# Leaving out the unread TensorE products at the tile edges of an LSTM and mixture-of-experts kernel

## The reference, cut to what matters

```python
def step(carry, xw_t):                       # L0: 1024 steps, one after the other
    prev_h, prev_c = carry
    a = xw_t + prev_h @ Wh                   # [2, 256] @ [256, 1024]
    i, f, o = sigmoid(three quarters of a); g = tanh(the last quarter)
    next_c = f * prev_c + i * g
    next_h = o * tanh(next_c)
x = x + hs
# L1: 2 shared experts, 8 routed experts of which the router takes 2 per token
shared = mean_e((silu(x @ s_w1[e].T) * (x @ s_w3[e].T)) @ s_w2[e].T)
routed = sum_e(gelu(x @ r_w1[e].T) @ r_w2[e].T * gate[:, e])
x = x + (shared * 2 + routed) / 4            # in effect; all ten experts are computed
```

## Time and profile before

| | |
|---|---|
| timed runs, median (lowest to highest) | 1907.95 us (1906.42 to 1908.26), 3 runs |
| the profiled execution's own time | 1904.1 us |
| its span, first to last instruction | 1902.3 us |
| mean granted TensorE clock over the span | 0.997 |
| TensorE products | 1818.4 us busy (96%), 45672 records |
| TensorE weight loads | 1609.8 us busy (85%) |
| VectorE | 1540.1 us busy (81%) |
| ScalarE | 851.9 us busy (45%) |
| GpSimd | 123.4 us busy (6%) |

### The profile page before, as it was taken

The page is one execution under the profiler, slowest core; times in us unless marked ns, Lnnn a source line. Parts: engine busy times, 40 slices in busy tenths (PEclk is TensorE's granted clock), DMA queues, the critical chain, the costliest instruction groups (busy, mean ns, idle before and its releaser), DMA issues. The chain is left out here.

```text
span 1902.3 us, 111519 instructions
## 1 busy us (share of the span) xinstructions
PE 1818.4 (96%) x45672; PEld 1609.8 (85%) x45672; DVE 1540.1 (81%) x13274; ACT 851.9 (45%) x5545; POOL 123.4 (6%) x409
## 2 busy tenths in 40 slices
PE   8999999999999999999999999999999999999998
PEld 7888888888888888888888888888888888888887
DVE  7788888788888878888788888888888788887884
ACT  4564444444444444444444444444444444444442
POOL 0000000000000000000000000000000000000000
PEclk9999999999999999999999999999999999999999
DMA  6000000000000000000000000000000000000000
GB/s 247 4 3 4 4 6 4 7 4 4 6 4 7 4 4 7 4 7 4 7 4 4 7 4 7 4 4 7 4 7 4 7 4 4 7 4 6 4 4 7
DMA packets 7282, 20.86 MB, mean 11 GB/s; under 512 B 1136, under 2 KB 5616, under 8 KB 5872
## 3 DMA queue, kind: packets, MB, share of 16 engines
q1 hardware_dynamic: 6768, 13.73, 1.9%
HBM read 11.63 MB, written 2.10 MB: 7 GB/s over the span
## 5 line engine op out<-in xcount | busy, mean ns | idle before, releaser
L734 PE MATMUL gates<-hh,wh_hi 128*128 128x24 f16 x8192 | 784.9, 183 | 0.0
L734 PE MATMUL gates<-hh,wh_lo 128*128 128x24 f16 x8192 | 784.9, 183 | 0.0
L734 PEld LDWEIGHTS gates<-hh,wh_hi 128*128 128x128 f16 x8192 | 550.8, 96 | 0.0
L734 PEld LDWEIGHTS gates<-hh,wh_lo 128*128 128x128 f16 x8192 | 549.6, 95 | 0.0
L333 ACT ACTIVATE gates<-gates 128x4 f32<-128x4 f32 x1024 | 161.8, 158 | 839.3 <-DVE gates L597 822.4
L716 PEld LDWEIGHTS gates<-hh,wh_lo 128*128 128x128 f16 x8192 | 274.1, 96 | 276.1 <-DVE hh L623 270.2
L742 PE MATMUL gates<-hh,wh_small 128*128 128x2 f16 x8192 | 489.6, 164 | 0.0
L716 PE MATMUL gates<-hh,wh_lo 128*128 128x24 f16 x8192 | 381.3, 185 | 73.0 <-DVE hh L623 10.5
L597 DVE TENSOR_TENSOR_SCAN gates<-part_fac,gates 128x8 f32<-128x8 f32 x2048 | 294.4, 178 | 168.0 <-PE gates L723 141.1
L723 PE MATMUL gates<-hh,wh_hi 128*128 128x4 f16 (+1 forms) x8192 | 370.4, 171 | 0.0
L742 PEld LDWEIGHTS gates<-hh,wh_small 128*128 128x128 f16 x8192 | 350.0, 96 | 0.0
(11 more groups left out here) (144 smaller groups left out, 2575.5 us busy)
## 6 DMA issues: line engine op xcount, KB each, us to landing
rw_sb<-rw SPq DMA_DIRECT2D x2, 2048.0 KB, 22.3
sw_sb<-sw SPq DMA_DIRECT2D x3, 1024.0 KB, 12.8
outT<-osb SPq DMA_DIRECT2D x16, 128.0 KB, 2.2
x_sb<-xT SPq DMA_DIRECT2D x1, 1920.0 KB, 8.9
wh_sb<-wh SPq DMA_DIRECT2D x1, 1024.0 KB, 4.8
wx_sb<-wx SPq DMA_DIRECT2D x1, 1024.0 KB, 6.3
x_sb<-xT SPq DMA_DIRECT2D x1, 128.0 KB, 4.6
eye_sb<-eye SPq DMA_DIRECT2D x1, 64.0 KB, 5.1
```

The lines of the kernel that those rows point to most:

```text
L734: mm(copies(q, m, LOW_COPIES)[:, :, :, 1], part, hh[:, c, half:half + 1, :].broadcast_to([P, LOW_COPIES, B]), start=False, stop=False, ski ...
```

## The change

The table `EDGE`, the helper `beside_up` and its call are taken out. Nothing else is altered: the same waits, the same order, the same other products.

```diff
 BETWEEN = (5, 8, 11, 14)
-EDGE = {0: 2, 1: 3, TS - 1: 3}
...
-            def beside_up(n):
-
-                for j in range(n):
-                    mm(up_sh[:, TT:BANK], wh_hi[:, 0, j * P:(j + 1) * P], wh_hi[:, 1, 0:BANK - TT], start=True, stop=True)
-
...
                 for s in range(TS):
                     lstm(s, it)
                     mixture(s, True)
-                    if s in EDGE:
-                        beside_up(EDGE[s])
                 take_back(pe, s_hhi, TS)
```

## The result

The change makes the kernel slower: 1921.03 us median of 4 runs (1918.28 to 1922.62) against 1907.24 us of the kernel before beside them (4 runs, 1906.42 to 1908.26), ratio 1.007 with a 95% interval of 1.0057 to 1.0083. 1915.8 us were predicted, with a range of 1905.2 to 1928. The profiled execution took 1922.29 us, its span is 18.2 us longer than the one before, and its mean granted clock is 0.978 instead of 0.997.

The account below looks back on a forecast made before the run. The prediction took each step's round through the engines, not TensorE alone, as the bound. Removing the products gains 2.2 us and half clock costs 10.1 us: +7.9 us, 1915.8 us with the timed offset, range 1905.2 to 1928.

Parts of the forecast that it names:

- What bounds the kernel: Each of 1024 steps is one round through the engines, 1.79 us; TensorE work ending before the next `hh` costs nothing.
- The direct gain: At 15 tile edges, removing step 1's three unread products saves 0.15 us each, 2.2 us; steps 63 and 0 give nothing.
- The price of a piece: A piece is 3.41 us of TensorE at half clock; priced at 0.84 us from a stretch in tile 0.
- The number of pieces: Half-clock stretches of 3.41 us newly expected around the 15 edges: 12, within 0 to 30, costing 10.1 us.
- Both sentences among the rivals on a second piece: At an edge, thinner half-clock steps favour a second 3.41 us half-clock stretch; float32 groups from step 2 on oppose it.
- The likeliest case: 8 to 22 half-clock stretches of 3.41 us, net of the 2.2 us gain: 1911.7 to 1924 us.
- The rival without a fall: Gate products alone keep TensorE's clock up at the edges; only 2.2 us gained, 1905.7 us; chance 0.22.
- Few falls: Only some edges lose the clock, 1 to 7 half-clock stretches, net -1.4 to +3.7 us, 1906.6 to 1911.6 us; chance 0.08.
- long falls everywhere: Two 3.41 us half-clock stretches at every edge, 30 in all, 1930.9 us; chance 0.10 for nearly every edge.
- The faster rival: Step 63's unread products also delay step 0 at each edge; 0.32 us per edge, 4.8 us, 1903.1 us; chance 0.04.

Follow-up runs that it names:

- e6: Kernel before with six instead of three unread products in step 1 of each edge; 1912.97 us, ratio 1.0045.
- e1: Kernel before without the three unread products of step 1 at each edge; 1902.01 us, ratio 0.9986.
- e2: Kernel before without the three unread products of step 63 at each edge; 1905.46 us, ratio 1.0002.
- e3: Kernel before without the two unread products of step 0 at each edge; 1905.16 us, ratio 1.0001.
- e7: Kernel before without step 1's unread products, plus eight 384-column unread products behind step 34 of tile 0; 1903.24 us, ratio 0.9991.
- e4: Kernel before with all eight unread products per edge cut from 384 to 24 columns; 1915.86 us, ratio 1.0067.
- e8: Kernel before with all eight unread products per edge cut from 384 to 192 columns; 1904.11 us, ratio 0.9999.
- e11: Kernel before with only step 63's three unread products kept at each edge; 1910.40 us, ratio 1.0017.
- e9: Kernel before with only step 0's two unread products kept at each edge; 1903.69 us, ratio 0.9996.
- e10: Kernel before without step 1's unread products, with unread 384-column products added at three waits (tile 0 start, step 34, behind tile 15); 1899.83 us, ratio 0.9971.
- e12: Kernel before with only step 1's three unread products kept at each edge; 1918.21 us, ratio 1.0046.

## Why the prediction was right, point by point

**What bounds the kernel: right.** The round of a step sets the pace. Work on TensorE in the gap is free up to 0.34 us beyond the logits in step 1 and costs one to one after that (e6).

**The direct gain, 0.15 us per edge from step 1 alone: right.** -0.20 and -0.13 us at the two edges of the kernel after that kept the clock, and 1.78 or 1.79 us instead of 1.94 for the step at all 15 edges of e1. The groups of steps 63 and 0 cost nothing, by e2 and e3.

**The price of a piece, 0.84 us: right at the edges, wrong in the tail.** An edge with one piece is 0.68 us longer, that is 0.83 with the 0.15 gained; one with two 1.44 us, 1.59 with it, or 0.80 a piece. The two pieces behind tile 15 cost 2.7 us, 1.4 each. In all traces what follows the last L623 takes 36.7 us without a piece, 37.9 to 38.2 with one, 39.2 to 39.4 with two. There the mixture runs alone, and I read the higher price as that of TensorE setting the pace itself, which no run tries. I had priced all pieces by a stretch of the recurrence. Its fourth step takes 1.86 us even at full clock (e7), so the piece there was 0.80 us rather than 0.84.

**The number of pieces, 12: too small, and this is the term that was mis-sized.** The profiled execution has 21: 19 at the edges (7 x 0.83 + 6 x 1.59 = 15.3 us) and two in the tail. With them 15.3 + 2.7 - 2.2 = 15.8 us; 1.3 us of longer set-up and 0.4 in tile 0 are the rest but 0.7. Between the medians it is 13.8 us where 7.9 were forecast. The 12 weren't derived but chosen between 0 and 30; that the time fell inside the range is owed to the range's width as much as to the mechanism. Both sentences among the rivals on a second piece had a share in it: six of 13 edges had two, where the fall came early and half clock lay over steps 0 to 2, and seven had one, where it came late and step 2's float32 groups followed. Nearly every edge fell, too, though in the profiled execution the first two did not. The likeliest case was put at 1911.7 to 1924 us for 8 to 22 pieces; by its own prices 8 pieces are 1912.5.

**The rival without a fall: wrong.** It rested on busy time, 1.87 us or more against 1.81. The fall at 606 us came after 2.19 us of work in 3.40, more than the 2.10 us that were not followed by one in the earlier trace rows. The one at 493.40 us came after 2.88 us. Busy time doesn't tell; what the runs show is that eight products of 24 columns left falls at six edges where eight of 384 or 192 columns left none (e4, e8). The rule of the Trainium skill (TensorE: Matmul & The Clock Gate, "Why this matters for your kernels") that leads to this rival, that a long idle gap brings the clock down, doesn't account for these falls: the longest gap ahead of the one at 606 us was 0.79 us, ahead of the one at 489.85 us in e11 it was 0.43, and e2 had 0.79 without a fall.

**Few falls, long falls everywhere, faster: none came.** 1930.9 us would have needed two pieces at every edge. The faster rival needed the group of step 63 to delay the tile's end; e2 excludes it.

**Open.** Why edges 1 and 2 of the profiled execution kept their clock while the later ones lost it was not tried; the runs at clock 0.976 to 0.980 say that others have some more or fewer pieces. That e7, e8 and e9 gain less in time than their steps show is put down to the tail and the set-up of the profiled executions only. Which of its two effects kept the clock in e7, and so in tile 0 of e10, is open.

## What to carry to other kernels

An unread product can earn its place on an engine that isn't the bound, because that engine's products are in the round that is, and they take longer at half clock. Ask of such filler how wide it is and where it stands: two wide products in the middle of the light stretch did here what eight narrow ones didn't, and what three at either end of it didn't. Ask also what stands right behind it: the last group cost 0.16 us for each product that ended too late, and more when the clock was down. Before taking filler out, look for the pieces at half clock that the trace has already and read their price there, once where the engine is waited for and once where it sets the pace.

## What the runs showed of the hardware

- A loss that isn't additive. Any one of the three groups can go for nothing; two can go if step 0's stays (e1, e2, e3, e9: 0.9986 to 1.0002); with all gone it is 13.8 us.
- A pattern that feeds itself. From edge 4 on the falls of the kernel after alternate, one piece, two pieces, one piece, and the stretches with two begin at 601.89, 833.99, 1066.09, 1298.19 and 1530.29, each 232.10 us after the last. In before two tiles take 229.9 us. In e12 every second edge falls, from the third on. I read this so: a fall lengthens the tile and with it moves the next edge against the throttle. No run shifts an edge by itself to show it. Either way a count of falls from one trace is not a chance that can be taken edge by edge.
- The granted clock had only the two levels, 1.00 and 0.50, in every record, and every stretch at 0.50 that ended inside the span lasted 3.41 or 6.83 us. At an edge it was two pieces when it began early and one when it began late (18 and 14 falls, above).
- The price of half clock depends on what sets the pace: 0.24 us for each us at an edge (0.80 to 0.83 us a piece), 0.40 in the tail (2.7 us for 6.83).
